# Narrower selections for the visits, and four visits to a cleared PSUM bank

## The reference

```
weight = einsum('rb,bio->rio', comp_l, bases_l);  h = einsum('ni,rio->nro', x, weight)
msg  = h[src, etype]
norm = 1 / max(count of edges with the same (dst, etype), 1)
agg  = segment_sum(msg * norm[:, None], dst, N)
x    = agg + x @ root_l + bias_l      # batch norm and relu behind layers 0 and 1
```

## Time and profile before

| | before |
|---|---|
| runs | 5345.99, 5364.67, 5364.16 us; median 5364.16 |
| profiled execution | 5356.81 us, its span 5354.7 us |
| granted TensorE clock, mean | 0.826 |
| busy: TensorE / weight loads | 3940.1 / 1992.2 us |
| busy: VectorE / ScalarE / GpSimd | 3231.6 / 1109.8 / 2710.8 us |

### The profile page before, as it was taken

The page is one execution under the profiler, slowest core; times in us unless marked ns, Lnnn a source line. Parts: engine busy times, 40 slices in busy tenths (PEclk is TensorE's granted clock), DMA queues, the critical chain, the costliest instruction groups (busy, mean ns, idle before and its releaser), DMA issues.

```text
span 5354.7 us, 66549 instructions
## 1 busy us (share of the span) xinstructions
PE 3940.1 (74%) x14160; PEld 1992.2 (37%) x14160; DVE 3231.6 (60%) x8826; ACT 1109.8 (21%) x1906; POOL 2710.8 (51%) x2646
## 2 busy tenths in 40 slices
PE   7017676777767777777777867777777669999997
PEld 3013343333333333343333333333333334444443
DVE  6965455444445666666666466666666676455464
ACT  4000000000013333333333433333333340000000
POOL 0666677676652666666666066666666610000000
PEclk9556666656668888989888988898888979999998
DMA  6011111111125444444444534444444438888895
GB/s 230 6 35 45 47 46 46 46 47 46 46 68 192 123 120 122 125 122 125 121 123 125 218 110 124 123 124 124 124 122 122 124 95 300 297 288 296 291 300 164
DMA packets 416155, 716.49 MB, mean 134 GB/s; under 512 B 98515, under 2 KB 322056, under 8 KB 415535
## 3 DMA queue, kind: packets, MB, share of 16 engines
q1 hardware_dynamic: 331562, 544.93, 30.1%
q0 software_dynamic: 84096, 166.09, 12.3%
q10 hardware_dynamic: 130, 1.20, 0.1%
HBM read 431.85 MB, written 279.93 MB: 133 GB/s over the span
## 4 chain that ended last, share of the span: by engine, by line
PE 58%; issue 16%; POOL 8%; DVE 7%; another core or an unknown queue 6%; DMA 3%; ACT 1%; SPq 1%; DVEq 0%; POOLq 0%; ACTq 0%
PE psum L936 20%; PE psum L923 11%; PE psum L984 7%; PE psum L985 7%; PE psum L912 6%; POOL area L604 6%; PE psum L883 3%; POOL key_list L574 3%; DMA area<-msg_table,visit_src 2%; PE psum L898 1%; DVE agg_and L1645 1%; DVE edge_area L1163 1%; DVE area L1615 1%; PE psum L999 1%
## 5 line engine op out<-in xcount | busy, mean ns | idle before, releaser
L604 POOL DMA_INDIRECT area<-msg_table,visit_src x2490 | 2530.2, 1016 | 1419.0 <-issue 600.7
L936 PE MATMUL psum<-area 128*128 128x256 f32 x4980 | 1904.9, 483 | 341.0 <-DMA area<-msg_table,visit_src 127.3
L936 PEld LDWEIGHTS psum<-area 128*128 128x128 f32 x4980 | 1023.8, 234 | 861.3 <-issue 566.9
L1645 DVE TENSOR_TENSOR agg_and<-agg_and,psum 128x256 f32 x1245 | 522.3, 420 | 1204.9 <-PE psum L936 539.8
L654 ACT CAST bufE<-psum 128x512 f16<-128x512 f32 x1507 | 883.3, 586 | 1666.5 <-PE psum L923 796.6
L923 PE MATMUL psum<-bufE,carry 128*128 128x512 f16 x1506 | 634.3, 421 | 677.4 <-issue 503.4
L1615 DVE TENSOR_SCALAR area<-iota,agg_and 128x256 f32<-128x256 f32 x2490 | 884.4, 417 | 14.2 <-ACT agg_and L670 12.6
L984 PE MATMUL psum<-area,edge_area 128*128 128x512 f16 (+1 forms) x1911 | 691.1, 369 | 16.2 <-DMA area<-counts 9.0
L985 PE MATMUL psum<-area,edge_area 128*128 128x512 f16 (+1 forms) x1911 | 690.6, 369 | 0.0
L923 PEld LDWEIGHTS psum<-bufE,carry 128*128 x1506 | 148.0, 98 | 1324.6 <-issue 1308.9
L912 PE MATMUL psum<-bufE 128*128 128x512 f16 x1507 | 627.1, 416 | 2.0 <-remote 0.7
(11 more groups left out here) (326 smaller groups left out, 1904.2 us busy)
## 6 DMA issues: line engine op xcount, KB each, us to landing
area<-counts SPq DMA_DIRECT2D x252, 896.0 KB, 4.5
counts<-bufE SPq DMA_DIRECT2D x1507, 128.0 KB
msg_table<-area SPq DMA_DIRECT2D x147, 512.0 KB, 2.6
area<-msg_table,visit_src POOLq DMA_INDIRECT x2490
agg_and<-counts SPq DMA_DIRECT2D x162, 128.0 KB, 4.5
area<-counts SPq DMA_DIRECT2D x21, 224.0 KB, 3.3
bufE<-inv_sqrt SPq DMA_DIRECT2D x2, 1568.0 KB, 11.3
out<-cur SPq DMA_DIRECT2D x12, 256.0 KB
```

The lines of the kernel that those rows point to most:

```text
L604: g.indirect_dma_start(out=msg[:, n % MV, :], out_offset=None, in_=msg_table, in_offset=bass.IndirectOffsetOnAxis(ap=visit_src[:, v:v + 1] ...
L936: t.matmul(psum[:, banks[c % len(banks)], at:at + W2], msg[:, n % MV, :], visit_sel[:, n % SV, :], start=v % 2 == 0, stop=v % 2 == 1).then ...
L1645: v.tensor_tensor(to, to, psum[:, banks[c % len(banks)], at:at + W2], ALU.add).then_inc(visit_added, 1)
```

## The change

Each visit's selection is 128 columns, the destinations of its own block. The four visits of a chunk share one whole PSUM bank of 512 columns, which stands for four blocks from that of the first visit on: TensorE first clears the bank with a product of zeros (`start=True`), and then each visit accumulates 128 columns at a place in the bank: the first at column 0, the others at 128 times the low two bits of their distance in blocks from it. VectorE adds the whole bank to 512 columns of `agg` at once. The correction of destinations to the pair's block in `keep_visits` is dropped. `visit_pack` holds two chunks to a word, 12 bits for each: 6 for the first visit's block, 2 for each other one's distance. TensorE reads it too, eight words at a time (PACKS), once in 16 chunks. `agg_and` is 256 columns wider.

```diff
-W2 = 256
+PACKS = 8
...
-        visit_sel = staging.rearrange("p (s n) -> p s n", n=W2)
+        visit_sel = staging[:, 0:SV * 128].rearrange("p (s n) -> p s n", n=128)
...
-        def pairs(k, q=0):
-            return NV // 2 * k + q
+        def chunks(k, c=0):
+            return NQ * k + c
...
+        def shifted(pack, by):
+            return (pack << -by) if by < 0 else (pack >> by)
+
+        def chunk_column(pack, c):
+
+            return shifted(pack, 12 * (c % 2) - 7) & (COLS - 128)
+
+        def visit_column(pack, c, j):
+
+            return shifted(pack, 12 * (c % 2) + 6 + 2 * (j - 1) - 7) & (BW - 128)
...
+                packs = [None]
+
+                def columns_of(c):
+
+                    if c % (2 * PACKS) == 0:
+                        first = c // 2
+                        packs[0] = nc.values_load_multi_w_load_instructions(
+                            visit_pack[0:1, first:min(first + PACKS, NVW)], engines=(mybir.EngineType.PE,))[1]
+                    pack = packs[0][c // 2 % PACKS]
+                    return [0] + [visit_column(pack, c, j) for j in range(1, len(chunk_of(c)))]
...
                 def sums(c):
                     blocks = list(built(k, c))
+                    columns = columns_of(c)
+                    bank = banks[c % len(banks)]
                     if c >= len(banks):
 
-                        pe.wait_ge(visit_added, pairs(k, pairs_of(c - len(banks))[-1] + 1))
-                    for v in chunk_of(c):
+                        pe.wait_ge(visit_added, chunks(k, c - len(banks) + 1))
+                    t.matmul(psum[:, bank, :], zeros16[:, 0:128], zeros16[:, :], start=True, stop=False, skip_group_check=True)
+                    for j, v in enumerate(chunk_of(c)):
                         n = visits(k, v)
-                        at = v % CH // 2 * W2
+                        to = psum[:, bank, bass.ds(columns[j], 128)] if j else psum[:, bank, 0:128]
+                        if j:
+                            pe.compute_val(columns[j] * 4)
                         pe.wait_ge(visit_ready, n + 1)
                         pe.wait_ge(visit_in[n % MV], visit_loads(k, v))
-                        t.matmul(psum[:, banks[c % len(banks)], at:at + W2], msg[:, n % MV, :], visit_sel[:, n % SV, :],
-                                 start=v % 2 == 0, stop=v % 2 == 1).then_inc(visit_summed, 1)
+                        t.matmul(to, msg[:, n % MV, :], visit_sel[:, n % SV, :], start=False, stop=v == chunk_of(c)[-1],
+                                 skip_group_check=True).then_inc(visit_summed, 1)
...
-                step, other = block_step, elsewhere
-                block_of = visit_dst.rearrange("p (q j) -> p q j", j=2)
-                link(v.memset(step, 0.0))
-                link(v.tensor_tensor(step.rearrange("p (q j) -> p q j", j=2)[:, :, 1], block_of[:, :, 1], block_of[:, :, 0], ALU.subtract))
...
-                link(v.scalar_tensor_tensor(out=step, in0=step, scalar=128.0, in1=visit_dst, op0=ALU.mult, op1=ALU.add))
-                link(v.tensor_scalar(other, visit_dst, 128.0, NODST, ALU.is_ge, ALU.mult))
-                link(v.tensor_tensor(step, step, other, ALU.add))
-                link(v.tensor_scalar(other, visit_dst, 0.0, NODST, ALU.is_lt, ALU.mult))
-                link(v.tensor_tensor(visit_dst, step, other, ALU.add))
...
-                        v.tensor_scalar(to, iota[:, 0:W2], low, norm[:, at:at + 1], ALU.is_equal, ALU.mult).then_inc(visit_ready, 1)
+                        v.tensor_scalar(to, iota[:, 0:128], low, norm[:, at:at + 1], ALU.is_equal, ALU.mult).then_inc(visit_ready, 1)
...
-                    for q in pairs_of(c):
-                        column, at = pair_column(pack, q), q % 2 * W2
-                        if pairs(k, q):
-                            dve.wait_ge(visit_added, pairs(k, q))
-                        to = agg_and[:, bass.ds(column, W2)]
-                        v.tensor_tensor(to, to, psum[:, banks[c % len(banks)], at:at + W2], ALU.add).then_inc(visit_added, 1)
+                    if chunks(k, c):
+                        dve.wait_ge(visit_added, chunks(k, c))
+                    to = agg_and[:, bass.ds(chunk_column(pack, c), BW)]
+                    v.tensor_tensor(to, to, psum[:, banks[c % len(banks)], :], ALU.add).then_inc(visit_added, 1)
```

More of the change, by code:

```diff
@@ L255, in build @@
         runs = bufE[:, 0:VB * 384].rearrange("p (j e w) -> p j e w", j=VB, w=3)
-        block_step, elsewhere = (bufE[:, VB * 384 + j * NVP:VB * 384 + (j + 1) * NVP] for j in range(2))
         tall = cur[:, 0:64 * CK].bitcast(BF16).rearrange("p (k m) -> p k m", m=128)
@@ L407, in chunk_of @@
             return range(CH * c, min(CH * c + CH, NV))
-        def pairs_of(c):
-            return range(CH // 2 * c, min(CH // 2 * c + CH // 2, NV // 2))
-        def pair_column(pack, q):
-            by = 6 * (q % 4) - 7
-            return ((pack << -by) if by < 0 else (pack >> by)) & (COLS - 128)
+        def shifted(pack, by):
[4 more added lines that the diff above has]
+            return shifted(pack, 12 * (c % 2) + 6 + 2 * (j - 1) - 7) & (BW - 128)
         def last_of_tiles(to, words, w):
@@ L1050, in _ @@
             degree(zeros16[0:EP, 0:NBLK], zeros16[0:EP, 0:128], start=False, stop=True).then_inc(degrees, 1)
-            pe.wait_ge(visit_added, pairs(LAYERS))
+            pe.wait_ge(visit_added, chunks(LAYERS))
             for c in range(NB + 3):
@@ L1225, in plan_visits @@
                 link(last)
-                first_of = visit_dst[:, :].rearrange("p (q j) -> p q j", j=2)
-                four = first_of[0:1, :, 0].rearrange("p (c j) -> p c j", j=4)
+                four = visit_dst[0:1, :].rearrange("p (c j) -> p c j", j=CH)
                 dve.wait_ge(x_turned, NXT)
-                pack = cur[0:1, 0:NVW]
-                link(v.scalar_tensor_tensor(out=pack, in0=four[:, :, 3], scalar=64.0, in1=four[:, :, 2], op0=ALU.mult, op1=ALU.add))
-                link(v.scalar_tensor_tensor(out=pack, in0=pack, scalar=64.0, in1=four[:, :, 1], op0=ALU.mult, op1=ALU.add))
-                link(v.scalar_tensor_tensor(out=visit_pack[:, :], in0=pack, scalar=64.0, in1=four[:, :, 0], op0=ALU.mult, op1=ALU.add))
+                pack, base = cur[0:1, 0:NQ], cur[0:1, NQ:2 * NQ]
+                two = pack.rearrange("p (c j) -> p c j", j=2)
+                link(v.tensor_scalar(base, four[:, :, 0], 1.0 - 64.0 * 21.0, None, ALU.mult))
+                link(v.scalar_tensor_tensor(out=pack, in0=four[:, :, 3], scalar=4.0, in1=four[:, :, 2], op0=ALU.mult, op1=ALU.add))
+                link(v.scalar_tensor_tensor(out=pack, in0=pack, scalar=4.0, in1=four[:, :, 1], op0=ALU.mult, op1=ALU.add))
+                link(v.scalar_tensor_tensor(out=pack, in0=pack, scalar=64.0, in1=base, op0=ALU.mult, op1=ALU.add))
+                link(v.scalar_tensor_tensor(out=visit_pack[:, :], in0=two[:, :, 1], scalar=4096.0, in1=two[:, :, 0], op0=ALU.mult, op1=ALU.add))
             def find_slots(step, buckets, counts, starts, number):
@@ L1658, in visit @@
                         plan_step(c)
-                dve.wait_ge(visit_added, pairs(k + 1))
+                dve.wait_ge(visit_added, chunks(k + 1))
             def split_group(hop, m):
```

4 lines of the change are left out of this document (2 added, 2 removed).

## The result

The changed kernel takes 5398.81 us (median of 5 runs, 5386.09 to 5401.71), the kernel before 5363.18 in the same comparison: ratio 1.0067, 95% interval 1.0052 to 1.0083. I had said 5250. The change makes the kernel 36 us slower, so even the sign of the forecast was wrong.

The account below looks back on a forecast made before the run. Gathers were taken to pace layer 0, the carry chain (high clock) or TensorE's streaming (low clock) layers 1 and 2. Gains 34 + 31 + 20 + 20 + 5 = 110 us off 5357 gave about 5250, range 5070 to 5420.

Parts of the forecast that it names:

- Registers: TensorE's queue: three or four operations per computed column, about 0.14 us, taken as covered; 261 us with no cover.
- the 0.11 us gap: TensorE's waiting in each 1.13 us high-clock period; with 0.20 us saved on the visit product, room for register work.
- Narrow products at the low clock: Layers 1 and 2: visit with a block falls from 1.71 to 1.44 us, saving 34 and 31 us.
- the rest: Layers 1 and 2, high clock: 77 visits without a block and a few more, 0.14 us each, 10 a layer.
- the carry chain: Carry product, ScalarE's copy, weight load: 1.13 us, ends last at high clock; estimated 1.34 at low clock after the change.
- Layer 0: Gathers pace the stage; shorter VectorE work may cut waits, bounds 0 and 112 us, 20 taken.
- Preparation: Before GpSimd's first gather: operations of 832 columns go, two small packing operations come; net gain 5 us.
- VectorE's selection: VectorE, each visit: selection falls from 415 ns to about 0.21 us; worth nothing in layers 1 and 2.
- D: Sequencer rival: register work uncovered in half the visits, 130 us, giving 5375; chance 0.22 together with B.
- B: Clock rival: less streaming keeps TensorE's clock low, blocks cost 1.44 not 1.13 us, up to 5620; chance about 0.16.
- C: Rival: stores and carry chain take the gain back, ScalarE's remote waits grow; about 5340; chance 0.14.
- A: Rival: visit product bound wherever the chain of waits shows it, periods under 1.13 us; about 5040; chance 0.17.

Follow-up runs that it names:

- h2: Changed kernel without the gathers of every second visit after the first sixteen (wrong sums), so that TensorE binds; 4047.35 us.
- h1: Kernel before without the gathers of every second visit after the first sixteen (wrong sums), so that TensorE binds; 4055.21 us.
- h4: Changed kernel with half the gathers left out, fixed columns and no register work for the visits (wrong sums); 3960.66 us.
- e1: Changed kernel with the four visits at fixed columns, no register work on TensorE (wrong sums); 5330.83 us, ratio 0.9941 to the kernel before.
- h3: Changed kernel with half the gathers left out and the next visit's register work ahead of the carry product's wait (wrong sums); 4004.64 us.
- e5: Changed kernel with the next visit's register work moved ahead of the carry product's wait, on a fast chip; 4872.74 us, ratio 0.9895 to the kernel before.
- e10: The kernel of e5 timed again, beside the changed kernel on a fast chip; 4878.56 us, ratio 0.9923 to the kernel before.
- j1: Kernel before, unaltered, run on a fast chip for its trace; 4915.85 us (one run).
- e9: Changed kernel, unaltered, timed again on a fast chip; 4881.19 us, ratio 0.9926 to the kernel before.

## Why the prediction was wrong, point by point

- **Registers: "Cost taken: 0" is the step that failed.** It costs 44 and 41 us in layers 1 and 2 where TensorE binds, 36 and 35 on the chip of the result. I put three or four operations at 36 ns, "about 0.14 us", from the duration in the earlier trace rows, and let the 0.11 us gap and the 0.20 us saved cover them. The 36 ns were right as a duration (L950: minimum, median and maximum 36 ns on a fast chip) and wrong as a price. In h2 the instructions between the carry product's weight load and the visit's start about 0.1 us apart: two operations, a wait, a third operation that carries the other wait, then the load, where in the kernel before one wait stood. A visit with a column to work out is held up by 0.35 us. The Trainium skill ("Perfetto Trace Analysis", Sequencer-only Instruction) says that the profile reports only the execution of such an instruction, and not its fetch, its wait or the push behind it; the trace agrees, with 36 ns reported and 0.097 from start to start.
- **The cover holds in the period that I had looked at, and not in the other.** In periods with one visit and one block nearly all of the 0.35 us is hidden, as forecast. The 157 periods with two visits have no room for it. I had put the visits without a block down for a gain of 0.14 each, and without register work they give it (h1 to h4, 224 to 196 us, 0.18 each); with it each costs 0.35 more. The same 0.11 us of gap was taken to cover every visit.
- **Narrow products at the low clock: 34 and 31, with 20 for the rest; measured 16 and 14 in all** (e1), 16 and 13 at the full clock (h4), where 28 of the 29 us lie in the periods with two visits: the "rest" came about as forecast, and the periods of one visit stay at 1.13. The product's size was right too: at the high clock its second record starts 0.108 us behind the first in 1107 of the 1212 visits that e1 did wholly at that clock in layers 1 and 2, so 0.22 for a visit and not 0.32. So was the low-clock period: the median of one visit and one block, without clearing or degree counts, is 1.66 us in the kernel before, 1.39 in the changed kernel and 1.34 in e1, the 1.34 being what I had worked out for the carry chain; with clearing it stays at 1.66. What failed is that the number of such periods stood still in my sum. The time at the low clock rose from 298 to 369 us in e1's layer 1 and from 279 to 362 in layer 2. At 1.34 us against 1.13 that is an estimated 71 / 1.34 x 0.21 = 11 and 13 us, 24 of the 55 that were missing; the rest stays open.
- **Layer 0: a gain of 20; measured a loss of 4.** The narrower work is worth 50 us there in h2, but only where the gathers don't bind, and with all of them they bound the layer on both kinds of chip.
- **Preparation: 5; measured 6.7.** Right.
- **The sum.** In place of 65 + 20 + 20 + 5 = 110 the terms came out as 30 for the narrower products in all, -71 for the register work, -4 and +7: -38, and the kernel lost 36.
- **VectorE's selection: 0.21 us; measured 0.36 alone and 0.28 in a row of four.** The row that I took (L1097) has a mean of 282 ns for one; I had divided the merged busy time by the count; the add was right (0.68 against 0.687). Nothing depended on either.
- **The rivals.** D, "register work uncovered", was the right one, down to its sign in the trace ("gaps ahead of the visit's weight loads while everything waited for is there"). I priced it at 130 us off the gain, 5375, and gave it little of the 0.22 that it shared with B; it took 71. B has a share as well: the clock stayed over the 0.8 that I had named as its sign, but in the changed kernel the time at the low clock rose by 94 and 161 us, and at 1.39 us a period against 1.13 that is an estimated 18 and 30 us, which is of the size of the loss of 42. C's "remote" waits fell, from 237.8 to 105.0 us. A is out: no period is under 1.13 us in any trace. (The floor of 1098 us that I gave GpSimd was too high: on fast chips layers that stand on the gathers took 1077.)

What is shown: register work makes the layers slower with the clock at 1.00 (h2), and without it the kernel gains at the lower clock too (e1). What stays open: how much of the 21 us per layer on the chip of the result the lower clock adds, for no run there held it up; and whether early register work makes the whole kernel better there. From h3, 22 and 20 us would come off 5399: an estimated 5357, level with the kernel before. On fast chips the kernel of e5, in e10, and the changed kernel are the same (0.9923 and 0.9926), both ahead of the kernel before. No version here is shown to beat both on both kinds of chip.

## What to carry to other kernels

Price a register or semaphore instruction by the distance from start to start in the queue (0.097 us here), not by its duration, and count the waits that the change splits off. Put it ahead of the wait that the queue stands in anyway; that gave half of its price back. Before a cost is taken as covered, look for the periods that have no slack: 157 of 1498 carried nearly two thirds of it. And don't hold the share of low-clock time fixed when the change takes streaming away. Before a gain on one engine is summed, ask which stages stand on another engine at all, on the chip at hand: the same change was a loss of 0.7% on one and a gain of 0.7% on others. And look in the trace whether an added cost is there before its time is read.

## What the runs showed of the hardware that I had not expected

- **The same kernel differs by 8% from chip to chip.** The kernel before took 5362 us on one and 4910 to 4927 on three others, with the same bytes and packets. (Whether that is the chip itself or a state that it was in isn't shown.) In layer 1 the gathers' queue was busy for 16.6% of 1252 us there and 19.6% of 1097 here, 208 and 215 us: the transfers aren't slower. Of the 441 us between the profiled executions 427 lie in the three visit stages. What differs there is waiting: in the whole trace ScalarE waits 497 us and GpSimd 201 us for "remote" on the one chip, and neither does in j1; the traces give no reason. In layer 0 of the kernel before VectorE's add waits 233.0 us for "remote" on the one chip (31 times, up to 17.1 us), and not at all in j1.
- **TensorE's queue has a slow gait of 0.70 us per instruction** on that chip. The register work of the changed kernel there, in layer 1 (count, ns minimum, median, maximum), and the same line in e9 on a fast chip:

```profile
L950 PEldq ALU_OP  x1400: 2/36/725, 1723.1 to 2992.6; - x175
```

```profile
L950 PEldq ALU_OP  x1400: 36/36/36, 1585.4 to 2663.4; - x175
```

  Counted over the three visit stages, 603 register and semaphore instructions of the queue took 0.68 to 0.72 us in the changed kernel, 33 in the kernel before and 22 in e1; none in j1 or e9. So on that chip they come with the register work. The price doesn't need them: h2 has not one stretch of them in layers 1 and 2 and pays more than the changed kernel there. What they cost on their own chip, no run shows. The Trainium skill ("Runtime: NRT & Kernel Launch", Instruction fetch mechanics) holds that fetching instructions is hidden behind their issue; whether these stretches are fetches that come late, no run here shows.
